# Weight pieces of stage three in halves, a paced split for stage six, and reordered ends of stage five

## The reference, cut to what matters

```python
x = x + L0_attn(layernorm(x))          # stage one: latent attention, 32 heads
x = x + L0_xattn(layernorm(x), ctx)    # stage two: attention to ctx, 8 groups of keys
x = x + L0_ffn(layernorm(x))           # stage three: x @ W_up + the LoRA of the chosen expert (top 1 of 4)
x = x + L1_attn(layernorm(x))          # stage four: 7 Taylor terms and a gated FFN of 1248 units
x = x + L1_xattn(layernorm(x), ctx)    # stage five: softmax(q k^T) v + skip, per sequence
x = x + L1_ffn(layernorm(x))           # stage six: relu(x W)^2 W2 + sum(top2 gates) * (x Wl We Wf), layernorm
```

```python
energy = jnp.einsum('bcn,bcm->bnm', q, k) / scale
x = jnp.einsum('bnm,bcm->bcn', jax.nn.softmax(energy, axis=-1), v)
return jnp.einsum('oc,bcn->bon', Wskip, pcd_up) + x
```

## Time and profile before

| | us |
|---|---|
| median of 3 runs | 1254.52 |
| lowest, highest | 1254.37, 1260.95 |
| the profiled execution, its time | 1251.37 |
| its span in the profile | 1249.6 |

### The profile page before, as it was taken

How to read it: one execution, slowest core, us unless ns; L and a number is a source line. 1 busy time by engine, 2 the same in 40 slices (tenths; PEclk the granted TensorE clock), 3 DMA queues, 4 the chain that set the end, 5 groups by cost and what they waited for, 6 DMA issues and landing times.

```text
span 1249.6 us, 23652 instructions
## 1 busy us (share of the span) xinstructions
PE 1109.9 (89%) x9380; PEld 594.0 (48%) x9380; DVE 738.6 (59%) x1255; ACT 464.2 (37%) x813; POOL 423.4 (34%) x365
## 2 busy tenths in 40 slices
PE   6798886988898789998799999999888799999992
PEld 3454453666664344444344444444455444444441
DVE  6777774788887674348613511532479833646456
ACT  4566562555555534321111211211256522223220
POOL 2355495788851320039500000000043300506053
PEclk9897995899999999999999999999999999999997
DMA  6000100111110111222100000000000000000000
GB/s 231 2 3 2 29 2 27 40 41 41 39 55 24 62 42 44 99 78 76 51 1 1 0 0 0 1 1 1 3 11 7 1 1 1 26 8 34 0 34 34
DMA packets 29011, 35.91 MB, mean 29 GB/s; under 512 B 5882, under 2 KB 20499, under 8 KB 28788
## 3 DMA queue, kind: packets, MB, share of 16 engines
q1 hardware_dynamic: 27506, 34.53, 8.4%
q10 hardware_dynamic: 1410, 0.06, 0.1%
HBM read 30.24 MB, written 4.19 MB: 28 GB/s over the span
## 4 chain that ended last, share of the span: by engine, by line
PE 58%; DVE 19%; issue 3%; ACT 3%; POOL 0%; DVEq 0%; ACTq 0%; POOLq 0%
PE p_up L116 10%; PE p_up L118 9%; PE p_up L117 9%; PE p_y L116 7%; PE p_y L118 7%; PE p_y L117 7%; DVE b_top L1355 2%; DVE wf_lo L241 2%; DVE e_den L2197 1%; PE p_y L1511 1%; ACT wd_hi L2246 1%; DVE e_top L2187 1%; PE p_up L110 1%; PE p_up L1499 1%; DVE d_term L1893 1%
## 5 line engine op out<-in xcount | busy, mean ns | idle before, releaser
L1902 DVE TENSOR_TENSOR d_h_low<-d_hf,d_h_high 128x512 f16<-128x512 f32 (+1 forms) x40 | 32.0, 799 | 199.9 <-ACT d_h_high L1979 199.9
L116 PE MATMUL p_up<-d_xt_high,wd_hi 128*128 128x512 f16 (+1 forms) x352 | 133.4, 379 | 2.9 <-PE p_y L118 1.5
L117 PE MATMUL p_up<-d_xt_low,wd_hi 128*128 128x512 f16 (+1 forms) x352 | 133.4, 379 | 0.0
L118 PE MATMUL p_up<-d_xt_high,wd_lo 128*128 128x512 f16 (+1 forms) x352 | 133.4, 379 | 0.0
L129 POOL TENSOR_SCALAR ve<-mv 128x4 f32<-128x4 f32 x16 | 4.9, 306 | 340.2 <-DVE mv L188 319.2
L116 PE MATMUL p_y<-wd_hi,d_h_high 128*128 128x512 f16 (+1 forms) x272 | 103.9, 382 | 9.1 <-DVE d_h_low L1902 9.0
L117 PE MATMUL p_y<-wd_lo,d_h_high 128*128 128x512 f16 (+1 forms) x272 | 103.8, 382 | 0.0
L118 PE MATMUL p_y<-wd_hi,d_h_low 128*128 128x512 f16 (+1 forms) x272 | 103.6, 381 | 0.0
L165 ACT ACTIVATE d_sg<-p_up 128x512 f32<-128x512 f32 (+1 forms) x40 | 23.8, 594 | 210.2 <-PE p_up L118 210.2
L430 POOL TENSOR_TENSOR a_pt_low<-a_ex,a_pt_high 128x1024 f16<-128x1024 f32 x32 | 68.2, 2131 | 75.1 <-ACT a_pt_high L919 75.0
L2460 DVE TENSOR_TENSOR d_h_low<-d_hf,d_h_high 128x512 f16<-128x512 f32 x32 | 27.5, 858 | 68.2 <-ACT d_h_high L2549 68.2
(11 more groups left out here) (331 smaller groups left out, 3023.6 us busy)
## 6 DMA issues: line engine op xcount, KB each, us to landing
wd_raw<-in_w_d SPq DMA_DIRECT2D x16, 616.0 KB, 3.5
wd_raw<-in_w_f SPq DMA_DIRECT2D x8, 578.0 KB, 3.5
X<-in_x SPq DMA_DIRECT2D x4, 1024.0 KB, 12.1
wd_lo<-in_ctx_t SPq DMA_DIRECT2D x128, 32.0 KB
out_x<-wd_raw SPq DMA_DIRECT2D x16, 256.0 KB, 2.0
wd_lo<-in_ctx SPq DMA_DIRECT2D x32, 64.0 KB, 2.3
wd_raw<-in_w_c SPq DMA_DIRECT2D x1, 1096.0 KB, 12.5
wd_hi<-in_Wo SPq DMA_DIRECT2D x1, 1024.0 KB
```

What stands on the lines that cost most here:

```text
L116: nc.tensor.matmul(ps, st[0], mv[0], start=start, stop=False)
L117: nc.tensor.matmul(ps, st[0], mv[1], start=False, stop=False)
L118: return nc.tensor.matmul(ps, st[1], mv[0], start=False, stop=stop)
L1902: nc.vector.tensor_tensor(hid[1][0:n, d % NH, :], value, hid[0][0:n, d % NH, :], ALU.subtract).then_inc(h_ready, 1)
```

## The change

Four edits.

1. In stage three ACT's two instructions for a weight piece are taken apart: the high part stays behind `norm` in iteration t, the scaling of the raw piece goes behind `norm` of iteration t + 1.
2. POOL waits for `h_ready` before each of stage six's eight pieces: pieces 0 to 4 for the low part of the blocks d = 7 to 11 of chunk 1, pieces 5 to 7 for those of d = 7 to 9 of chunk 2.
3. At the front of stage five DVE adds the last four tiles of stage four two by two (`add`), with tile 1's `soft` and tile 0's `total` between them, and takes the statistics of three of them (`measure`) after tile 1's `total`. POOL makes the `rstd` of this chunk after its second product instead of ahead of the first, and the split of the small weights `w2` moves from its tiles 1 and 2 to 2 and 3.
4. At the end of stage five DVE normalises stage six's first two tiles earlier: tile 0 after the `soft` of tile 14, tile 1 ahead of the `soft` of tile 15. Their transposes go to the banks 2 and 3 of `p_up` (`f.turned`), whose scores are read first, so PE makes them before it transposes tile 14; tiles 2 and 3 go to the banks 0 and 1. The transposes of tile 15 move behind the router products, and ACT's copies of tiles 14 and 15 behind the high parts of two tiles each.

```diff
@@ stage three, scalar
-            if t in EARLY:
-                weights(EARLY.index(t))
+            if t in EARLY:
+                weights[0](EARLY.index(t))
+            if t - 1 in EARLY:
+                weights[1](EARLY.index(t - 1))
@@ stage four, gpsimd
                 for q in range(NP_F):
                     part = slice(PF * q, PF * q + PF)
+                    pool.wait_ge(h_ready, DND + G6 + 2 + q if q < 5 else 2 * DND + G6 + 2 + q - 5)
                     split_piece(nc, pool, raw[:, q % 2, 0:PF], held.wf_hi[:, part], held.wf_lo[:, part],
                                 wf_in[q % 2], 16 * (q // 2) + 16, wf_split, 3 * q, held.apart)
...
-                for c in range(NC):
+                for c in range(NC - 1):
                     rstd_chunk(nc, pool, held, c, stats, held.rs_e + 2 * c)
@@ stage four, vector
+                def add(i):
+                    t = NT - TC + i
+                    v.wait_ge(y_ready, t + 1)
+                    nc.vector.scalar_tensor_tensor(held.X[:, t, :], p_y[:, i, :], 1.0 / (HS * WS), held.X[:, t, :],
+                                                   ALU.mult, ALU.add).then_inc(y_read, 1)
+
+                def measure(i):
+                    stats_tile(v, nc, held, NC - 1, i, y_read, NT - TC + i + 2, (held.apart, stats))
                 e.soft(v, 0)
-                update_one(NC - 1, 0)
-                update_one(NC - 1, 1)
+                add(0)
+                add(1)
+                e.soft(v, 1)
                 e.total(v, 0)
-                e.soft(v, 1)
-                update_one(NC - 1, 2)
-                update_one(NC - 1, 3)
+                add(2)
+                add(3)
+                measure(0)
                 e.total(v, 1)
+                for i in range(1, TC):
+                    measure(i)
@@ stage five, gpsimd
-            if t in (1, 2):
-                l = t - 1
+            if t == 1:
+                last_rstd(pool)
+            if t in (2, 3):
+                l = t - 2
@@ stage five, vector
             if w + 1 < NT:
                 norm(v, w + 1)
+            else:
+                norm_next(0)
...
+        norm_next(1)
         soft(v, NT - 1)
         update(v, NT - 3)
         total(v, NT - 1)
@@ stage five, scalar and tensor
-        values(act, NT - 2)
...
-        transposes(pe, NT - 2)
@@ stage six
+            f.turned = held.p_up[:, 2:4, :], held.p_up[:, 0:2, :]
...
-                norm(0)
-                norm(1)
+                norm_first(v, 2)
+                norm_first(v, 3)
                 low_x(0)
-                norm(2)
                 low_x(1)
-                norm(3)
                 e.update(v, NT - 2)
...
-                        if first and i == 1:
-                            e.values(act, NT - 1)
+                        if first and i % 2:
+                            e.values(act, NT - 2 + i // 2)
...
                     last.then_inc(logit_ready, 1)
+                    if first:
+                        e.transposes(pe, NT - 1)
...
-                pe.wait_ge(e.exp_ready, NT)
                 turn_one(0)
                 turn_one(1)
+                e.transposes(pe, NT - 2)
                 e.output(pe, NT - 2)
-                e.transposes(pe, NT - 1)
                 turn_one(2)
                 turn_one(3)
```

40 lines of the change are left out of this document (25 added, 15 removed).

## The result

The changed kernel takes **1234.85 us** (median of 4 runs, 1233.28 to 1240.67) where the kernel before takes 1254.85 in the same comparison (median of 4, 1254.37 to 1260.95): a ratio of 0.9841, 95% interval 0.9815 to 0.9867, 20.0 us less. The forecast was 1235.2 with 19.3 us less. The profiled execution of the changed kernel took 1236.02 us (span 1234.2), only 15.4 less than the profiled one of before. So I compare stretch by stretch; each is measured between two instructions that both programs have. What this text calls the start of stage three is the delta of its tile 1 (the first row of the table).

A forecast was written before the change was run, and what follows sets the result against it. PE bounds stage four, waiting in chunk 1 for DVE instructions held by POOL's splits; stage five is a DVE and ACT loop. 14.3 + 1.7 + 1.4 + 1.9 = 19.3 us less gives a 1235.2 us median; 1231 to 1240 at 68%.

The forecast's parts named there:

- The forecast case: Whole kernel: all four edits give about what was computed, 1231 to 1240 us; chance 68%.
- halves that escape the block: Rival, stage three: POOL's subtraction finds another place against `c_pick`, up to 6.1 us less instead of 1.7, 1230.8; chance 10%.
- Edit 2: Stage four: the second half of a chunk covers the pieces, chunk 1 becomes like chunk 2, 14.3 us less.
- the margin: Stage four, block d = 8: the low part is done 5.7 us before its down product starts.
- The slower rival: Second halves of chunks: PE waits per piece, 4.8 us each, 38.4 for eight, 1273.6 us; chance 4%.
- Edit 1: Stage three: thirteen intervals alternate between about 5.35 and 4.5 us, 62.8 instead of 64.56, 1.7 us less.
- The block of `c_pick`: Stage three: `c_pick` ends with POOL's subtraction, 1.06 us instead of 0.22, adding 0.84 to the next first half.
- Edit 3: Front of stage five: two additions without statistics end earlier, tile 2's `soft` starts at 911.0; 1.4 us less, between 0.4 and 2.5.
- The 0.2 us for the second weight split: Stage five: the second `w2` split, now beside a loaded tile, costs about 0.2 us.
- Edit 4: End of stage five: router products 4.6 us earlier, minus 1.09 for transposes and 1.7 for half clock; 1.9 us less, between 0 and 3.6.
- Norm 2 gets in: End of stage five: norm 2 runs ahead of POOL's product after the last reciprocal; norm 3 is held until that product ends.
- The edits don't touch what makes this difference: Whole time: the median's 3.15 us above the profiled execution stays, so 1232.1 profiled becomes 1235.2 median.

The follow-up runs named there:

- three other releases there: Changed kernel with POOL waiting only ahead of its first and sixth piece (1236.38 us), released by ScalarE's high part (1233.86 us), or by VectorE's `d_hf` (1233.29 us).
- the front alone: The kernel before with only the reordered front of stage five: 1255.01 us, ratio 0.9988.
- the reordered ends: Changed kernel with two statistics moved ahead of tile 1's sum and stage six's third norm behind two low parts: `e_top` 18.32 us, router products 7.11 us.

## Why the prediction was right, and where it was not

**The forecast case came**: 1234.85 against 1235.2, 20.0 us less against 19.3. The nearest rival in time, 1230.8 for halves that escape the block, lies only just outside the interval; what rules it out are the alternating intervals. That the median came within 0.4 us of the forecast is luck: single runs of the changed kernel lie between 1233.28 and 1240.67, and the edits' own stretches gave 2.0 us more than forecast, of which the beginning of stage four took back a part.

**Edit 2, right.** 14.86 us against 14.3; the edit alone gives the same chunk. That POOL stretches VectorE's instructions in a chunk's first half is shown by the release moved there (13.8 us lost), and that the second half covers the pieces by three other releases there, none of which costs anything. The prediction put the wait down to `d_h_low` alone, 9.0 us; its 14.3 held because it took the whole difference of the chunks, with the 3.3 us for `d_xn` and the 2.6 us of longer work in it. It set chunk 1 equal to chunk 2; chunk 1 is another 0.5 us shorter, since PE waits 0.6 us in it and 1.1 in chunk 2. One sign failed: I expected `d_h_low` of up to 3 us in the blocks d = 8 to 12 and there were none (0.75 at most), because the release puts each piece between two low parts. I had computed the margin and not the phase. The slower rival, PE waiting per piece, has no support: low parts held by 2.0 us reached no one.

**Edit 1, the mechanism right, the size too small, a part of it then lost.** Alternating intervals came, 4.44 and 5.21 to 5.29 instead of 4.5 and 5.35. Of the thirteen, 2 x 4.45 + 5 x (5.23 + 4.45) + 4.58 is 61.9: rounding each of the two up by 0.05 to 0.12 made 2.75 us into 1.7. The block of `c_pick` was confirmed by removing it. What the sum did not have is the beginning of stage four at half clock, 1.2 us in the mean of the traces. If that loss belongs to the halves, they are worth about 1.6 us, near the 1.7 by two errors that cancel; if not, they are worth 2.75.

**Edit 3, right.** `e_den` came 14.48 us behind the last scores of stage four (15.58 before), 1.10 less where 1.04 was forecast; `e_top` at 19.42, where 911.0 - 891.56 = 19.44 was forecast. The 0.2 us for the second weight split did not appear: the loop behind it took 80.13 us against 80.04, and 79.89 with the front alone.

**Edit 4, right in its sum, wrong in two steps.** Router products 4.8 us earlier (4.6 forecast), transposes between, and half clock behind the router products, which cost 0.9 us on the transposes and 1.0 on the latent products (1.7 forecast); 1.98 left (1.9). But the prediction had the clock drop behind the router products because of the idle time ahead of them. In the changed kernel it had fallen 5.2 us ahead of them, at 981.28, and stayed down; the kernel before has such a drop too, at 993.52. The cost came as forecast, the drop was an old one that lasted longer. "Norm 2 gets in" failed: norm 2 was held until POOL's product ended, as the reordered ends show. The forecast survived because norm 3 behind it costs 0.6 us only, and PE's transposes and ScalarE's high parts of both tiles follow one another in any case.

**From the profiled execution to the median.** "The edits don't touch what makes this difference" was right, and yet the profiled executions differ by 15.4 us only. The 3.15 us of before look like its luck in stages one and two (stage three started at 391.45, in no other trace so early) and at the front of stage five; its other runs have no profile that could show it. The profiled execution of after has 395.94 there and lies 1.2 us above its median. The forecast of 1232.1 for it missed by 3.9 us: 4.5 from stages one and two and 1.4 from stage four's beginning were missing in it, and the edits' own stretches gave 2.0 more than it had.

## What to carry to other kernels

A second engine's background work costs where it meets instructions whose lateness somebody waits for: find the stretch with the largest reserve, there blocks with 5.7 us in hand, and release one piece per block from an event just behind the instruction that it would hold. For the time the place was enough, also with the pieces back to back. Where two engines block each other, even a 128x8 copy lasts until the other's instruction ends (1.76 us instead of 0.17), so when an order is changed, look at what small instructions come under it. And compare two profiled executions by stretches between the same instructions: their whole spans differed here by 15.4 us where the medians differ by 20.0.

## What the runs showed of the hardware that I had not expected

- Of two instructions that become due together, the one whose row starts clearly earlier ran through: `d_h_low` 0.18 us ahead of POOL's scaling took its 0.69 us and POOL 0.40 more; a norm 0.16 us ahead of POOL's product took 0.50. But a norm whose row starts 0.06 us ahead was held until the end of the product and took 2.23 us.
- The Trainium skill ("SBUF — State Buffer", Who interferes with whom) says that whoever issues first has the shared pair for the whole instruction. By that rule the last case was issued second; the start times of the rows can't show this within 0.1 us.
- The granted clock of stages one and two, the same code in all programs, moves the start of stage three by up to 8.2 us from execution to execution, and PE's beginning of stage four by 1.4 us or more. The Trainium skill ("TensorE: Matmul & The Clock Gate", What's actually happening) says that the clock follows the array's recent activity. The rows agree where PE had been idle (at the end of stage five it waited 2.17 us ahead of 980.03, and the clock fell at 981.28), but the same 1.4 us of idle time ahead of stage four was followed by half clock in eleven traces and not in three.
